# First group of a cross-attention stream: front transfers queued anew, normalised columns made by two engines on two banks

## The reference, cut to what matters

```python
def _forward(x, xf_1, xf_2, ...):
    res = x
    h = _layer_norm(x, ln1_scale, ln1_offset)      # (x - mu) * rsqrt(var + eps) * scale + offset
    x = res + _cross_attention(h, xf_1, wq1, bq1, wk1, bk1, wv1, bv1, wo1, bo1, bias_k1, bias_v1)
    ...                                            # a second such attention, then an MLP
def _cross_attention(q_in, kv_in, wq, bq, ...):    # 16 heads of 128
    qh = (q_in @ wq + bq)                          # q from the normalised x
    kh = (kv_in @ wk + bk); vh = (kv_in @ wv + bv) # k and v from the context
    ...                                            # scores, softmax, ctx @ wo + bo
```

## Time and profile before

| | |
|---|---|
| runs, us | 1801.89, 1802.86, 1803.03 (median 1802.86) |
| profiled execution, us | 1800.83 |
| its span, us | 1799.1 |
| busy share PE / PEld / DVE / ACT / POOL | 94% / 80% / 52% / 55% / 30% |
| start of slot 0's q product, us | 21.23 |

### The profile page before, as it was taken

The page is one execution under the profiler, slowest core; times in us unless marked ns, Lnnn a source line. Parts: engine busy times, 40 slices in busy tenths (PEclk is TensorE's granted clock), DMA queues, the critical chain, the costliest instruction groups (busy, mean ns, idle before and its releaser), DMA issues. The chain is left out here.

```text
span 1799.1 us, 36043 instructions
## 1 busy us (share of the span) xinstructions
PE 1689.8 (94%) x14356; PEld 1444.5 (80%) x14356; DVE 938.7 (52%) x2064; ACT 995.4 (55%) x1932; POOL 545.7 (30%) x601
## 2 busy tenths in 40 slices
PE   6999999999999999999999889899989789987599
PEld 5988898889888889888988778767666567766598
DVE  6644444444455344444444464477859656667433
ACT  4545555555455455555555455477648667776444
POOL 4210000000053000000000153167844478766311
PEclk9999999999999999999999999999989999999699
DMA  5030000000000000000000010210010000001001
GB/s 171 20 121 16 8 23 23 7 17 23 25 1 25 24 1 23 23 23 0 23 23 0 1 30 1 56 49 2 2 22 1 7 1 2 1 13 30 1 12 35
DMA packets 59134, 40.02 MB, mean 22 GB/s; under 512 B 15725, under 2 KB 58262, under 8 KB 59030
## 3 DMA queue, kind: packets, MB, share of 16 engines
q1 hardware_dynamic: 54790, 34.90, 6.8%
q10 hardware_dynamic: 4240, 3.67, 0.7%
HBM read 36.46 MB, written 2.10 MB: 21 GB/s over the span
## 5 line engine op out<-in xcount | busy, mean ns | idle before, releaser
L580 ACT ACTIVATE l0a_weight_t<-l0a_t_ps 64x256 f32<-64x256 f32 x256 | 97.0, 379 | 270.3 <-PE l0a_t_ps L433 260.3
L730 DVE TENSOR_TENSOR l0a_c_lo<-l0a_c_ps,l0a_c_hi 128x512 fp32r<-128x512 f32 x128 | 88.5, 692 | 260.5 <-ACT l0a_c_hi L598 260.5
L768 DVE TENSOR_TENSOR x<-l0a_o_ps,x 128x1024 f32<-128x1024 f32 x64 | 78.4, 1225 | 211.9 <-PE l0a_o_ps L83 174.7
L315 POOL COPY l0a_head_bias<-l0a_bias_cols 128x2 f32 (+1 forms) x32 | 6.5, 202 | 492.4 <-DVE l0a_logit L718 491.0
L81 PE MATMUL l0a_o_ps<-l0a_wo_hi,l0a_c_hi 128*128 128x256 f32 x512 | 149.3, 292 | 4.3 <-DVE l0a_value_rows L704 2.9
L455 PEld LDWEIGHTS l0a_c_ps<-l0a_weight_t,l0a_v 128*128 128x128 f32 x1024 | 133.9, 192 | 14.1 <-ACT l0a_weights_t L583 2.9
L81 PE MATMUL l0a_v_ps<-l0a_wv_hi,ctx_hi 128*128 128x256 f32 x512 | 144.2, 282 | 0.0
L82 PE MATMUL l0a_o_ps<-l0a_wo_lo,l0a_c_hi 128*128 128x256 f32 x512 | 144.2, 282 | 0.0
L82 PE MATMUL l0a_v_ps<-l0a_wv_lo,ctx_hi 128*128 128x256 f32 x512 | 144.2, 282 | 0.0
L83 PE MATMUL l0a_o_ps<-l0a_wo_hi,l0a_c_lo 128*128 128x256 f32 x512 | 144.2, 282 | 0.0
L83 PE MATMUL l0a_v_ps<-l0a_wv_hi,ctx_lo 128*128 128x256 f32 x512 | 142.9, 279 | 0.0
(11 more groups left out here) (435 smaller groups left out, 4876.0 us busy)
## 6 DMA issues: line engine op xcount, KB each, us to landing
l0a_raw<-in_L_xattn_wq_dram SPq DMA_DIRECT2D x32, 128.0 KB, 2.3
l0a_raw<-in_L_xattn_wk_dram SPq DMA_DIRECT2D x32, 128.0 KB, 2.4
l0a_raw_v<-in_L_xattn_wv_dram SPq DMA_DIRECT2D x16, 256.0 KB, 3.3
l0a_raw_o<-in_L_xattn_wo_dram SPq DMA_DIRECT2D x32, 128.0 KB, 2.8
l3a_room<-in_L_xattn_wo_dram SPq DMA_DIRECT2D x2, 2048.0 KB, 8.4
l3a_room<-in_ctx_dram ACTq DMA_DIRECT2D x4, 512.0 KB, 10.1
l3a_room<-in_L_xattn_w_fc_dram SPq DMA_DIRECT2D x2, 1024.0 KB, 11.5
l3a_room<-in_ctx_dram SPq DMA_DIRECT2D x1, 2048.0 KB, 11.1
```

The lines of the kernel that those rows point to most:

```text
L315: pool.tensor_copy(head_bias[p][:], bias_cols[:, BQ:BK + 1, bass.ds(h, 1)].rearrange("p a b -> p (a b)"))
L580: last = act.activation(weight_t[half, :, :, b, :], t_ps[half, 0:GT // 2 * P] .rearrange("p (m b q) -> p m b q", b=HB, q=SEQ), ACT.Copy)
L730: dve.tensor_tensor(c[p][1][:], c_ps[:], c[p][0][:].bitcast(F32), ALU.subtract).then_inc(c_lo, 1)
L768: dve.tensor_tensor(chip.x[:, own, :], o_ps[:], chip.x[:, own, :], ALU.add).then_inc(added, 1)
```

## The change

Five things are done at once.

1. Queues. ACT now queues context group 0, the two weights of head 0, and the gains: five transfers in place of nine. Groups 1 to 3 of context and `x` go to SP's queue, behind `x` group 0, the five biases (moved ahead), the weights of head 1 and the v weights.
2. DVE normalises group 0 after only one lo chunk of context 0.
3. PE turns the rows of `x` group 0 right behind context 0, ahead of the biases and of context 1.
4. ACT makes `h_hi` of chunk 0 while DVE makes `whole` of chunk 1 (different banks), then they swap banks, each after the other has finished; DVE takes the biases and then both `h_lo`. Context 1's lo chunks come behind that. ACT splits the v weights ahead of head 1's.
5. Context 1's first chunk is turned into half of `o_ps` in place of `q_ps`, so that slot 0's q product no longer waits for it, and that product waits for `h_lo` chunk by chunk.

```diff
-        ctx_banks = (c_ps, v_ps, q_ps, k_ps, c_ps, t_ps, k_ps, k_ps)
+        ctx_banks = (c_ps, v_ps, half_banks[1], k_ps, c_ps, t_ps, k_ps, k_ps)
...
                 sp.dma_start(chip.x[:, group_rows(0), :], x_dram[:, group_rows(0), :]).then_inc(x_in[0], 16)
-                fetch_w(0, slice(0, K), 0)
+                fetch_biases(0)
                 fetch_w(0, slice(K, HP * K), 1)
                 fetch_v(0, slice(0, HP * K))
-                fetch_biases(0)
+                for g in range(1, NG):
+                    sp.dma_start(ctx_rows[:, group_rows(g), :], ctx_dram[:, group_rows(g), :]).then_inc(rows_in[g], 16)
+                    sp.dma_start(chip.x[:, group_rows(g), :], x_dram[:, group_rows(g), :]).then_inc(x_in[g], 16)
...
                         for ch in range(CH):
+                            if S == 0 and x == 0:
+                                pe.wait_ge(x_lo_done, ch + 1)
...
-                        if first_use(S) is not None:
+                        if first_use(S) is not None and S > 0:
                             pe.wait_ge(x_lo_done, CH * (first_use(S) + 1))
-                        if S == 0:
-                            pe.wait_ge(ctx_lo_done, 3)
...
                 for ch in range(CH):
                     turn_context(0, ch)
+                turn_rows(0, first_banks)
                 turn_biases(0)
...
-                turn_rows(0, first_banks)
...
                 act.dma_start(ctx_rows[:, group_rows(0), :], ctx_dram[:, group_rows(0), :]).then_inc(rows_in[0], 16)
+                for x, name in enumerate(("wq", "wk")):
+                    act.dma_start(raw[0][:, x, :, :], wt[0][name].rearrange("(c p) n -> p c n", p=P)[:, :, 0:K]).then_inc(raw_in[0], 16)
...
-                for g in range(1, NG):
-                    act.dma_start(ctx_rows[:, group_rows(g), :], ctx_dram[:, group_rows(g), :]).then_inc(rows_in[g], 16)
-                    act.dma_start(chip.x[:, group_rows(g), :], x_dram[:, group_rows(g), :]).then_inc(x_in[g], 16)
...
                 split_w(0, 0)
+                act.wait_ge(gain_in[0], 32)
+                for ch in range(CH):
+
+                    act.wait_ge(x_turned, CH)
+                    if ch == 1:
+                        act.wait_ge(x_whole_done, 1)
+                    act.activation(chip.h_hi[:, ch, group_columns(0)], first_banks[ch][:], ACT.Identity, bias=gain[:, 0, 1, ch:ch + 1],
+                                   scale=gain[:, 0, 0, ch:ch + 1]).then_inc(x_hi_done, 1)
                 for ch in range(CH):
                     take_context(1, ch)
-                take_rows(0, first_banks)
+                split_wv(0)
                 split_w(0, 1)
-                split_wv(0)
...
                 measure_group(0)
-                for ch in range(CH):
-                    rest_of_context(0, ch)
+                rest_of_context(0, 0)
                 normalise(0)
+                rest_of_context(0, 1)
+                dve.wait_ge(gain_in[0], 32)
+                for n, ch in enumerate((1, 0)):
+
+                    dve.wait_ge(x_turned, CH)
+                    if ch == 0:
+                        dve.wait_ge(x_hi_done, 1)
+                    dve.tensor_scalar(whole[:, ch, :], first_banks[ch][:], gain[:, 0, 0, ch:ch + 1], gain[:, 0, 1, ch:ch + 1],
+                                      ALU.mult, ALU.add).then_inc(x_whole_done, 1)
                 take_biases(0)
                 for ch in range(CH):
-                    rest_of_context(1, ch)
-                for ch in range(CH):
-                    take_whole(0, ch, first_banks[ch])
-                    dve.wait_ge(x_whole_done, ch + 1)
+                    dve.wait_ge(x_whole_done, CH)
+                    dve.wait_ge(x_hi_done, ch + 1)
                     dve.tensor_tensor(chip.h_lo[:, ch, group_columns(0)], whole[:, ch, :],
                                       chip.h_hi[:, ch, group_columns(0)].bitcast(F32), ALU.subtract).then_inc(x_lo_done, 1)
+                for ch in range(CH):
+                    rest_of_context(1, ch)
                 split_wv(0)
```

## The result

The changed kernel took 1798.1 us (median of 13 runs, 1796.65 to 1799.41), the kernel before 1801.96 on the same chip (13 runs, 1800.1 to 1803.03): ratio 0.9978, 95% interval 0.9971 to 0.9986. That is 3.9 us or 0.2% faster, and the interval leaves out 1. The time lies 0.1 under the range's lower end, 1798.2, and 2.3 under the forecast's 1800.4. The profiled execution took 1798.81 in a span of 1797.1: 2.0 less than the one before, where the forecast said 2.4.

What follows compares the result with a forecast made beforehand. PE bounds the kernel from 45 us, DVE's chain to group 1's rows the front. 5.2 at q − 0.6 (chain) − 1.2 (moved chunks) − 1.0 (clock) = 2.4 us off median 1802.86: 1800.5, stated 1800.4, range 1798.2 to 1802.8.

Steps and rivals of the forecast that it cites:

- knot: One of three holdups in the first 45 us: ACT's late start, the path to slot 0's q, group 1's rows.
- ACT's queue: Start of the program: five transfers in place of nine, queueing done near 3.5 us, table load near 4.8.
- the four rows: DVE normalising group 0: from 9.37 us, end between 10.8 and 12.0, taken as 12.0 with POOL's weight split among them.
- PE's idle time: Ahead of group 1's rows, after slot 0: PE waits 1.2 to 2.9 us, until about 24.2.
- DVE's chain: DVE's work up to group 1's rows: 3.4 us earlier, so 3.4 of the 5.2 at slot 0's q are left.
- − 1.0 for the clock: Slot 1: PE's idling may cost the high clock level, net 0.7 to 1.2 us, taken as 1.0.
- an idle of the upper half: PE's wait before group 1's rows in the upper half of 1.2 to 2.9 us, likelier to cost the high clock.
- rival B: Gain swallowed: DVE's line 640 (now 648) collides with POOL's split of head 1's weights, 1.2 us lost; 1802.3, chance 0.22.
- rival A's second form: Slot 1: the clock stays up, 3.4 to 4.6 us gained, 1799.5 to 1798.3; chance 0.27 for both forms.
- 1802.86 − 2.4: Whole kernel: median of the runs shown before, less the 2.4 us gain, gives 1800.5, stated as 1800.4.
- A's first form: Group 0: POOL's weight split stays behind all four rows, end 10.8; 3.6 us gained, 1799.3; chance 0.27 for both forms.
- C: Start of the program: context 1 lands late with all six big transfers in one queue, slower, 1806.5; chance 0.04.

Runs made afterwards that it cites:

- five profiles: The changed kernel, unedited, profiled in five executions: slot 2 started at 32.41 to 34.62 us, mean 33.1.
- the pair of executions above: Two profiled executions of the changed kernel, nothing edited: 1800.37 and 1796.92 us.
- the changed kernel with fillers: 20 unread transposes added on PE at the end of slot 0, ahead of group 1's rows, in the changed kernel: 1800.17 us, ratio 0.9989.
- the kernel with fillers ahead of slot 0: 14 unread transposes added on PE between group 0's rows and slot 0's q product, in the kernel before: 1802.32 us, ratio 1.0004.

## Why the prediction was right and wrong

**Right, step by step.** In the profile after, every knot but q, which was 0.4 late, fell within 0.3 of where the rows of before put it: ACT's queue (table load 3.73), the four rows with POOL's split among them (2.33, end 11.76), the turning, `h_lo`, line 648, group 1's rows, PE's idle time. DVE's chain, not q, set what came through: of 4.84 at q, 2.42 were left at slot 2. The Trainium skill, page "SBUF — State Buffer", section "Who interferes with whom", has the shared ports held for a whole instruction by whoever issued first. The trace agrees: the row that came due during POOL's split took 1.35 in place of 0.40, and the four ended at 11.76, not near 10.8.

**The step that failed: "− 1.0 for the clock".** I wrote that the high level "may come before k is through" and took only the outcome that follows from it, an idle of the upper half and a fall, for every execution. It happened in two of five profiles. In the other three the high level came at 20.4 to 21.6, the idle was under 0.9, and slot 2 started 1.3 sooner. The first row of the argument, PE at 0.42 a matmul in slot 0, was the state of these three. Where the fall comes, its price was about right (1.3 and 1.0 for 1.0); as a mean over the five it is some 0.5. Group 1's rows end 3.2 earlier in the mean, where the forecast had 3.4, as rival B's collision took 1.1 off in one of the five. 3.2 less 0.5 gives the 2.8 of the five profiles, against the forecast's 2.4, and rival A's second form ("the clock stays up", 3.4) named the cases that it left out. The runs say 3.2 ± 0.5; the 0.4 between that and 2.8 lies within their error, and no experiment accounts for it.

**The base, which moved the time more.** "Against the median it is 1802.86 − 2.4": the three runs shown lay above the mean of all 112 of the same kernel, 1801.5. Of the 2.3 by which the measured 1798.1 lies under 1800.4, 1.3 is this base, 0.4 the clock term as the five profiles have it, and the remaining 0.6 is chance or not explained. With the base at 1801.5 the same forecast gives 1799.1. The profiled execution, 1800.83, was a somewhat nearer base than that median. Runs of the kernel before spread over 5.5 us, and the pair of executions above shows how much of such a spread can arise behind 1025 us, which no front can touch.

**Rivals.** B's mechanism was seen and cost 0.9 to 1.1 in its execution, not the whole gain. A's first form, POOL's split behind all four rows, was not seen (end 11.76), and C's was not: context 1 had landed by 11.5. The rows show that the change does what it says. How often each kind of front comes stays open, as five profiles are few, and so does what decides when the high level comes in one and the same program. Open too is why the changed kernel with fillers, whose profiled front was within 0.2 of the shortest, had a mean time 0.9 above the changed kernel's; its 11 runs and the spread of 1.2 don't settle it.

## What to carry to other kernels

Before a front is priced, find the next engine in line and what it will wait for: here 4.8 us at slot 0's first product were 2.8 at slot 2, and a collision further down (POOL's zeroing beside DVE's rows) held as much again. Moving work that nobody awaits out of the way of a chain that everybody awaits was one edit of two lines, and worth 2.6 us on top of the change's 3.2; in the kernel before it gave 0.7 at slot 2. And where the clock's state is part of the sum, price both states and profile one program several times, since a single profile shows one of them.

## What was not expected of the hardware

- The granted clock rose at 15.4 in two executions of the changed kernel and at 20.4 to 21.6 in three others, with the same instructions at the same times to 0.1 us up to the start of q. Ahead of the falls seen in slot 1, PE had stood idle for 2.73, 3.78 and 3.45, and in the kernel with fillers ahead of slot 0 for 1.58, after which the rows came one by one (2.20 for eight transposes in place of 1.32); behind idles of 0.38 to 0.88 there was none.
- When POOL's and DVE's work on two areas of SBUF each comes due within 0.04 us, either can be the one that is stretched: DVE 0.69 and POOL 1.87 in the profile after, DVE 1.80 and POOL 1.30 in the next, from the same program. By the recorded starts POOL was first in both, by 0.03 and 0.04, so these starts don't tell which of the two is stretched.
- POOL's small copies of the turned biases took 0.67 beside DVE's `h_lo` and 0.20 alone (19.31 in the profile after), and the end of the second is what ended the 0.77 of idle time ahead of q.
